# Six-layer macaron block on one core: GpSimd scales the normed rows behind the routed layers, kept rows go straight to their place, and the first combine loop is reordered

## The reference, cut to what matters

```
def _layernorm(x, axis=-1, eps=1e-05):
    m = jnp.mean(x, axis=axis, keepdims=True)
    v = jnp.var(x, axis=axis, keepdims=True)
    return (x - m) / jnp.sqrt(v + eps)
...
x = L0_attn_x
x = x + 0.5 * _L0_ffn_ref(_layernorm(x, axis=-1), ...)    # routed: 8 experts, top 2
x = x + _L0_attn_ref(_layernorm(x, axis=-1), ...)         # selective scan
x = x + 0.5 * _L0_ffn_ref(_layernorm(x, axis=-1), ...)    # routed again
x = x + 0.5 * _L1_ffn_ref(_layernorm(x, axis=-1), ...)    # soft: 64 experts, 32 slots each
x = x + _L1_attn_ref(_layernorm(x, axis=-1), ...)         # gated linear attention
x = x + 0.5 * _L1_ffn_ref(_layernorm(x, axis=-1), ...)    # soft again
```

## Time and profile before

| | before |
|---|---|
| median of 3 runs | 2232.11 us (2231.87 to 2232.35) |
| the profiled execution, own time | 2253.2 us |
| its span | 2251.4 us, 24417 instructions |
| mean granted TensorE clock | 0.954 of full speed |
| busy: TensorE, VectorE, ScalarE, GpSimd | 1869.9, 1666.6, 1184.8, 1230.3 us (83%, 74%, 53%, 55%) |
| chain that ended last, by engine | TensorE 35%, VectorE 32%, "issue" 15%, GpSimd 9%, ScalarE 4%, DMA 2% |
| of it, VectorE's scaling L1156 | 2% |

### The profile page before, as it was taken

One profiled execution on the slowest core, in us unless ns is written; L12 is line 12 of the kernel. 1 busy time (PEld: TensorE's weight loads), 2 busy tenths in 40 slices (PEclk: granted clock), 3 DMA queues, 4 the chain that ended last, 5 costly groups with the idle time before them and its releaser, 6 DMA issues.

```text
span 2251.4 us, 24417 instructions
## 1 busy us (share of the span) xinstructions
PE 1869.9 (83%) x6046; PEld 907.8 (40%) x6046; DVE 1666.6 (74%) x2166; ACT 1184.8 (53%) x2820; POOL 1230.3 (55%) x796
## 2 busy tenths in 40 slices
PE   4099686888888833986999999998987999999998
PEld 3067532333333521764333344443333433344443
DVE  5223488999999840327999967886687999958886
ACT  2322186555555332215999854332456999963332
POOL 3734307999999564552999800000785999900000
PEclk9999898999999956998999999999899999999999
DMA  7123293455455111325000000000650300000000
GB/s 261 50 84 103 94 154 113 169 178 176 169 176 176 64 60 51 107 71 169 1 0 0 1 1 1 0 0 0 186 141 19 94 0 0 0 1 5 9 9 14
DMA packets 102320, 163.63 MB, mean 73 GB/s; under 512 B 11008, under 2 KB 65843, under 8 KB 102113
## 3 DMA queue, kind: packets, MB, share of 16 engines
q1 hardware_dynamic: 94050, 146.41, 22.0%
q0 software_dynamic: 8192, 16.30, 2.0%
HBM read 125.09 MB, written 38.14 MB: 73 GB/s over the span
## 4 chain that ended last, share of the span: by engine, by line
PE 35%; DVE 32%; issue 15%; POOL 9%; ACT 4%; DMA 2%; another core or an unknown queue 1%; DVEq 1%; POOLq 0%; SPq 0%; ACTq 0%
PE ps L2005 10%; DVE arena L1461 5%; PE ps L1737 5%; PE ps L1750 5%; DVE arena L1523 5%; DVE arena L1467 5%; DVE arena L1459 4%; PE ps L1876 4%; PE ps L2033 3%; POOL arena L575 2%; POOL arena L638 2%; DVE arena L1529 2%; DVE arena L1406 2%; DVE stage L1156 2%; POOL arena L600 1%
## 5 line engine op out<-in xcount | busy, mean ns | idle before, releaser
L1951 PE MATMUL ps<-arena 128*128 128x512 f32 x512 | 250.6, 612 | 13.9 <-POOL arena L600 13.8
L608 POOL TENSOR_TENSOR arena<-arena 128x864 f32<-128x864 f32 x128 | 210.1, 1642 | 80.2 <-DVE arena L1459 77.4
L1942 PE MATMUL ps<-c_phiT,arena 128*128 128x512 f32 x512 | 244.1, 600 | 5.8 <-DVE arena L1461 3.8
L2005 PE MATMUL ps<-XT,c_phiT 128*128 (+1 forms) x512 | 243.4, 593 | 3.9 <-DVE arena L1499 3.9
L600 POOL TENSOR_TENSOR arena<-arena 128x1024 f32<-128x1024 f32 x128 | 246.6, 1928 | 0.0
L2033 PE MATMUL ps<-arena 128*128 128x512 f32 x512 | 227.7, 604 | 11.2 <-DVE arena L1529 11.2
L638 POOL TENSOR_TENSOR arena<-arena 128x1024 f32<-128x1024 f32 x32 | 63.6, 2000 | 299.2 <-DMA arena<-value_rows 299.2
L538 POOL DMA_INDIRECT token_outputs<-arena x128 | 124.3, 971 | 151.0 <-DVE arena L1298 112.0
L889 ACT ACTIVATE arena<-arena 128x32 f32<-128x32 f32 x640 | 195.7, 311 | 0.0
L1406 DVE TENSOR_TENSOR_SCAN arena<-ps,arena 128x1024 f32<-128x1024 f32 x84 | 187.9, 2274 | 6.4 <-POOL arena L570 6.2
L1876 PE MATMUL ps<-arena,c_ident 128*128 128x512 f32 x336 | 161.0, 601 | 28.3 <-POOL arena L575 28.3
(11 more groups left out here) (241 smaller groups left out, 3711.7 us busy)
## 6 DMA issues: line engine op xcount, KB each, us to landing
arena<-input_gates SPq DMA_DIRECT2D x128, 512.0 KB, 3.8
arena<-value_rows SPq DMA_DIRECT2D x32, 512.0 KB, 5.0
arena<-slot_inputs SPq DMA_DIRECT2D x32, 258.0 KB
arena<-in_L_ffn_w SPq DMA_DIRECT2D x32, 256.0 KB
arena<-token_outputs SPq DMA_DIRECT2D x16, 512.0 KB, 6.7
slot_inputs<-arena SPq DMA_DIRECT2D x1, 4128.0 KB, 13.4
slot_inputs<-zero SPq DMA_DIRECT2D x1, 4128.0 KB, 33.5
token_outputs<-arena SPq DMA_DIRECT2D x1, 4096.0 KB
```

Of the source, the lines that this page charges most:

```text
L608: pool.tensor_tensor(Ed[:, r, PSLOT * NA:].rearrange("p (n q) -> p n q", q=PSLOT), Lc[:, r, PSLOT * NA:].rearrange("p (n q) -> p n q", q=P ...
L1942: ins = pe.matmul(pbank(2 * h + c), xts[:, r // 2, :], phiT[:, at:at + CHUNK], start=True, stop=True)
L1951: ins = pe.matmul(pbank(4 + 2 * h + c), xns[:, r // 2, :], Dd[:, r, CHUNK * c:CHUNK * (c + 1)], start=start, stop=stop, skip_group_check=True)
L2005: ins = pe.matmul(pbank(t % 4), phiT[:, P * t:P * (t + 1)], xt(b, c), start=True, stop=without_m)
```

## The change

Three things are changed.

1. Kept rows (n = 0, 2, 3) are scaled straight into `XN[:, t, 0:D]`, TensorE turns them from there, and the 24 copies by ScalarE (L687) go, with the semaphore ln_keep; GpSimd's dispatch waits for ln_x instead.
2. Behind the routed layers (n = 1 and n = 3) the 32 scalings of each norm (8 chunks of 4 tiles) move from VectorE to GpSimd, behind its last scatter and, in layer 0, ahead of the clearing of `dts`.
3. In the combine loop of s = 0, VectorE's statistics use fixed slots and bn_aggr, `ln_apply` moves behind `weigh` and `tree`, TensorE's `ln_turn` behind `total` and `turn_y`, and ScalarE's `ln_copies` behind `finish`. In the loop of s = 1 `residual` moves behind `weigh` and `tree`.

```
@@ GpSimd, experts
-                    hold(pool, sem("ln_keep"), CHUNKS * m + c1)
+                    hold(pool, sem("ln_x"), 16 * m + c1)
...
                 store(E // 2 - 1, False, True)
 
+                n = 2 * m + 1
+                for c in range(CHUNKS):
+                    hold(pool, sem("ln_rstd"), 8 * n + c + 1)
+                    if m == 0 and c >= 2:
+                        pool.wait_ge(sem("ln_T"), 8 * n + c - 1)
+                    for j in range(PER_CHUNK):
+                        t = PER_CHUNK * c + j
+                        normed = XN[:, t, 0:D] if m else stage[:, c % 2, D * j:D * (j + 1)]
+                        ins = pool.tensor_scalar(normed, X[:, t, :], ln_s[:, 4, t:t + 1], ln_s[:, 7, t:t + 1], ALU.subtract, ALU.mult)
+                    ins.then_inc(sem("ln_x"), 1)
@@ ScalarE
-                if n in KEPT:
-                    hold(act, sem("ln_x"), 8 * n + c + 1)
-                    act.activation(XN[:, ds(4 * c, 4), 0:D], stage[:, h, :].rearrange("p (j d) -> p j d", d=D),
-                                   ACT.Copy).then_inc(sem("ln_keep"), 1)
...
                         copy_y(v - 1)
+                        finish(v)
                         if s == 0:
                             ln_copies(4, i - 1, c, 7)
-                        finish(v)
@@ VectorE, norms
-                if not (isinstance(v, int) and v < 2):
+                if n not in KEPT:
                     dve.wait_ge(sem("ln_T"), v - 1)
-                    if n in KEPT and not (isinstance(c, int) and c < 2):
-                        dve.wait_ge(sem("ln_keep"), 8 * KEPT.index(n) + c - 1)
...
+                    normed = XN[:, t, 0:D] if n in KEPT else stage[:, h, D * j:D * (j + 1)]
@@ VectorE, statistics (in a hardware loop seven operations before)
-                dve.tensor_tensor(two_mean, even(1), odd(1), ALU.add)
...
-                dve.tensor_tensor(var, var0, gap2, ALU.add).then_inc(sem("ln_var"), 1)
+                for t in range(at, at + PER_CHUNK):
+                    ins = dve.bn_aggr(ln_s[:, 4:6, t], stats[:, t, :])
+                ins.then_inc(sem("ln_var"), 1)
@@ VectorE, behind a routed layer
                     ln_statistics(2 * m + 1, grp)
-                    if grp:
-                        ln_apply(2 * m + 1, grp - 1, (grp - 1) % 2)
-                ln_apply(2 * m + 1, CHUNKS - 1, 1)
@@ VectorE, combine loop
                         less_m(v, c)
+                        weigh(v - 1, 1 - c, 1)
+                        tree(v, c)
                         if s == 0:
                             ln_apply(4, 2 * (i - 1) + c, c)
                         else:
                             residual(v - 2, i - 1, c)
-                        weigh(v - 1, 1 - c, 1)
-                        tree(v, c)
@@ TensorE, combine loop
                         combine(v - 1, 1 - c, False)
+                        total(v)
+                        turn_y(v - 1, False)
                         if s == 0:
                             ln_turn(4, 2 * (i - 1) + c, c, 7)
-                        total(v)
-                        turn_y(v - 1, False)
```

More of the change, by code:

```diff
@@ L672, in _, with ln_scale @@
             act.preload_act_table_set("natural_log_exp_and_others")
-            def ln_scale(n, c):
+            def ln_scale(n, c, ring=None):
+                at = 4 * (c if ring is None else ring)
                 hold(act, sem("ln_var"), 8 * n + c + 1)
-                act.activation(ln_s[:, 6, ds(4 * c, 4)], ln_s[:, 5, ds(4 * c, 4)], ACT.Ln, bias=eps[:, :]).then_inc(sem("ln_ln"), 1)
+                act.activation(ln_s[:, 6, at:at + 4], ln_s[:, 5, at:at + 4], ACT.Ln, bias=eps[:, :]).then_inc(sem("ln_ln"), 1)
                 hold(act, sem("ln_ln"), 8 * n + c + 1)
-                act.activation(ln_s[:, 7, ds(4 * c, 4)], ln_s[:, 6, ds(4 * c, 4)], ACT.Exp, scale=-0.5)\
+                act.activation(ln_s[:, 7, at:at + 4], ln_s[:, 6, at:at + 4], ACT.Exp, scale=-0.5)\
                     .then_inc(sem("ln_rstd"), 1)
@@ L933, in exp_T @@
                         if before and t == ST - 4:
-                            ln_scale(4, 2 * before[0] + before[1])
+                            ln_scale(4, 2 * before[0] + before[1], before[1])
                         hold(act, sem("LT"), ST * v + t + 1)
@@ L976, in soft @@
                     ln_copies(4, BATCH - 1, 0, 7)
-                    ln_scale(4, CHUNKS - 1)
+                    ln_scale(4, CHUNKS - 1, 1)
                     ln_copies(4, BATCH - 1, 1, 7)
@@ L1118, in _, with ln_statistics @@
             chain(dve.memset(XT[:, :, 0:CONV_PAD], 0.0))
-            def ln_statistics(n, c):
-                v = 8 * n + c
+            def ln_statistics(n, c, ring=None):
+                at = 4 * (c if ring is None else ring)
                 for j in range(PER_CHUNK):
-                    ins = dve.bn_stats(stats[:, ds(4 * c + j, 1), :].rearrange("p a b -> p (a b)"),
-                                       X[:, ds(4 * c + j, 1), :].rearrange("p a b -> p (a b)"))
-                if isinstance(v, int):
-                    ins.then_inc(sem("ln_step"), 3)
-                    dve.wait_ge(sem("ln_step"), 3 * v + 3)
-                    for t in range(4 * c, 4 * c + 4):
-                        ins = dve.bn_aggr(ln_s[:, 4:6, t], stats[:, t, :])
-                    ins.then_inc(sem("ln_var"), 1)
-                    return
-                ins.then_inc(sem("ln_step"), 1)
-                dve.wait_ge(sem("ln_step"), 3 * v + 1)
-                even, odd = (lambda j: stats[:, ds(4 * c, 4), j]), (lambda j: stats[:, ds(4 * c, 4), 3 + j])
-                two_mean, gap, m2, gap2, mean, var, _, _, var0 = (ln_s[:, j, ds(4 * c, 4)] for j in range(9))
-                dve.tensor_tensor(two_mean, even(1), odd(1), ALU.add)
-                dve.tensor_tensor(gap, even(1), odd(1), ALU.subtract)
-                dve.tensor_tensor(m2, even(2), odd(2), ALU.add).then_inc(sem("ln_step"), 1)
-                dve.wait_ge(sem("ln_step"), 3 * v + 2)
-                dve.scalar_tensor_tensor(gap2, gap, 0.25, gap, ALU.mult, ALU.mult)
-                dve.tensor_scalar(mean, two_mean, 0.5, None, ALU.mult)
-                dve.tensor_scalar(var0, m2, 1.0 / D, None, ALU.mult).then_inc(sem("ln_step"), 1)
-                dve.wait_ge(sem("ln_step"), 3 * v + 3)
-                dve.tensor_tensor(var, var0, gap2, ALU.add).then_inc(sem("ln_var"), 1)
+                    ins = dve.bn_stats(stats[:, at + j, :], X[:, ds(4 * c + j, 1), :].rearrange("p a b -> p (a b)"))
+                ins.then_inc(sem("ln_step"), 1)
+                hold(dve, sem("ln_step"), 8 * n + c + 1)
+                for t in range(at, at + PER_CHUNK):
+                    ins = dve.bn_aggr(ln_s[:, 4:6, t], stats[:, t, :])
+                ins.then_inc(sem("ln_var"), 1)
             def ln_apply(n, c, h):
@@ L1149, in ln_apply @@
                 dve.wait_ge(sem("ln_rstd"), v + 1)
-                if not (isinstance(v, int) and v < 2):
+                if n not in KEPT:
                     dve.wait_ge(sem("ln_T"), v - 1)
-                    if n in KEPT and not (isinstance(c, int) and c < 2):
-                        dve.wait_ge(sem("ln_keep"), 8 * KEPT.index(n) + c - 1)
+                at = 4 * (h if n == 4 else c)
                 for j in range(PER_CHUNK):
                     t = 4 * c + j
-                    ins = dve.tensor_scalar(stage[:, h, D * j:D * (j + 1)], X[:, ds(t, 1), :].rearrange("p a d -> p (a d)"),
-                                            ln_s[:, 4, ds(t, 1)], ln_s[:, 7, ds(t, 1)], ALU.subtract, ALU.mult)
+                    normed = XN[:, t, 0:D] if n in KEPT else stage[:, h, D * j:D * (j + 1)]
+                    ins = dve.tensor_scalar(normed, X[:, ds(t, 1), :].rearrange("p a d -> p (a d)"),
+                                            ln_s[:, 4, at + j:at + j + 1], ln_s[:, 7, at + j:at + j + 1], ALU.subtract, ALU.mult)
                 ins.then_inc(sem("ln_x"), 1)
@@ L1665, in ln_turn @@
                 for j in range(PER_CHUNK):
-                    ins = pe.transpose(pbank(bank)[:, P * j:P * (j + 1)], stage[:, h, P * j:P * (j + 1)], ident[:, :])
+                    normed = XN[:, 4 * c + j, 0:D] if n in KEPT else stage[:, h, P * j:P * (j + 1)]
+                    ins = pe.transpose(pbank(bank)[:, P * j:P * (j + 1)], normed, ident[:, :])
                 ins.then_inc(sem("ln_T"), 1)
```

4 lines of the change are left out of this document (2 added, 2 removed).

## The result

| | before | changed |
|---|---|---|
| median of 15 runs each | 2234.01 us (2230.89 to 2236.52) | 2236.85 us (2234.81 to 2238.53) |
| ratio to before, 95% interval | | 1.0015 (1.0009 to 1.0022) |
| the profiled execution, own time | 2253.2 us | 2236.5 us |
| its span | 2251.4 us | 2234.7 us |

The change makes the kernel 0.15% slower; 2209 was predicted, 1.0% faster. In a second comparison on another occasion the ratio was 1.0017 (1.0008 to 1.0026).

A forecast was written before the change was run, and what follows sets the result against it. TensorE and VectorE were taken to share the path, VectorE bounding the norm behind routed layer 0. Gains 9.8 + 5.4 + 4.0 + 3.6 = 22.8 us gave 2209.3 us; main-case range 2204 to 2216, wider range 2200 to 2225.

The forecast's parts named there:

- one input less makes the memset the nearer row, so I take 0.3: Norms behind routed layers: GpSimd's scaling of one 128-column tile estimated at 0.3 us, between 0.11 (memset) and 0.62 (additions).
- the formula for layer 1: Gain behind routed layer 1 if GpSimd sets the pace at s per scaling: 21.1 - 32s; layer 0's is 26.4 - 32s.
- Gain 9.8 behind layer 0: Norm behind routed layer 0: TensorE becomes the pace, first Silu at 280.75 against 290.5; 9.8 us, 3.3 from the memset stall.
- gain 5.4 behind layer 1: Norm behind routed layer 1: last turn and copy end at 1041.5 against 1046.97; 5.4 us (4.5 to 5.9).
- Loops, 4.0 and 3.6: Soft layers' combine loops: scaling (first) and residual (second) leave the path ahead of the tree; 4.0 and 3.6 us.
- The loops give nothing: Rival on the combine loops: TensorE refills the supposed path, so only 15.2 us remain, 2217; chance 0.04.
- Kept rows, nothing: Norms whose rows are kept: dropping 24 ScalarE copies of 0.63 us gains nothing, as ScalarE idles or copies beside TensorE's turn.
- the second rival: Slow GpSimd scaling in the norms behind routed layers: total gain 55.1 - 64s, 2258 at s = 1.27; chance 0.06.
- GpSimd is slow: Rival on the norms behind routed layers: scaling price s turns the gain to zero at 0.86, 2258 at 1.27; chance 0.06.
- GpSimd holds VectorE: Rival on the norms behind routed layers: each GpSimd scaling also stops VectorE; 8.1 us gained in all, 2224; chance 0.12.
- The stalls of the dispatch vanish: Rival on both routed layers' dispatch: the edit removes two waits of 7.26 us, 14.5 us more gained, 2195; chance 0.05.
- The memset beside the taps: Behind routed layer 0: memset now beside VectorE's convolution taps, counted as costing 0, with 2.4 us kept for the range.

The follow-up runs named there:

- residual_only: Kernel before, with only the residual moved behind the second product and the tree in the second soft layer's combine loop; 2226.12 us, ratio 0.9976.
- drain_ahead: Changed kernel, but GpSimd signals the end of routed layer 1 with its drain ahead of the 32 scalings; 2228.80 us against 2232.11, ratio 0.9986.
- wide_ahead: Changed kernel with two 128x512 tensor_tensor per chunk for GpSimd's scaling and its barrier drain ahead of the scalings; 2214.56 us against 2232.13, ratio 0.9924.
- wide: Changed kernel, but GpSimd scales a chunk by two tensor_tensor of 128x512 instead of four tensor_scalar of 128x128; 2241.74 us against 2257.45, ratio 0.9936.
- dve_both: Changed kernel with the scalings behind both routed layers on VectorE again; 2222.89 us, ratio 0.9960 to the kernel before.
- columns: Changed kernel, GpSimd scaling 64 columns per instruction behind layer 0 and 512 behind layer 1 (wrong scalars there), for the price alone; single run 2241.91 us.

## Why the prediction was wrong

- **The step that failed: "one input less makes the memset the nearer row, so I take 0.3".** Measured: 0.775 from one to the next. In the prediction's own sum this alone turns the 15.2 us of the two norms into a loss of 2.1. Of the 25.6 us between the forecast and the result that is 17.3; the drain (below) is 5.4 and the late projections about 2.5. The error lies in the choice of the near rows: a memset reads nothing, an addition has no scalars, and both bounds (0.11 and 0.62) were below the price. An instruction's form had a price that no row of before held, and the far bound of 1.27 was the only honest upper one. With 0.775 the formula for layer 1 is right: 21.1 - 32 x 0.775 is -3.7, and the scaling cost 3.6. The one for layer 0 gives 26.4 - 24.8 = 1.6 up to the first Silu. From the first addition to it the changed kernel took 31.5, against 32.5 in the profiled execution of before, but against 30.8 in residual_only, which has the code of before there. So the formula was 0.6 to 2.3 too favourable, since its rows came from an execution with a lower clock in that stretch. And 0.775 has a second cost that the formula leaves out, 2.4 to 2.8 us behind the first Silu (scan start minus first Silu: 81.9 against 79.1 to 79.5), where TensorE's projections start late and at the clock of 0.50; with wide scalings, at 1.00, this cost is gone (79.3).
- **The wait that was not seen: GpSimd's drain at the barrier.** The prediction let the soft layer start 2.2 us after the last scaling. To ask what is queued behind the scalings on GpSimd would have found it: `stage_end` stood there, and in the trace of before GpSimd's drain was done 27 us ahead of ScalarE's last copy (1019.79 and 1046.97), so it cost nothing. 5.4 us, shown by drain_ahead.
- **Gain 9.8 behind layer 0** came out as a loss of 3.4 to 3.8, **gain 5.4 behind layer 1** as a loss of 9.0. With both causes mended (wide_ahead) the same two stages gain 6.1 and 2.3 against residual_only, which has the old code there: the mechanism (VectorE relieved, TensorE nearly the pace) was right, and the size was too large by 3.7 and 3.1. Of the 3.7, 1.7 is the low clock in the execution that the forecast started from. In both stages the turns come 2.4 apart and not 2.2, with waits for GpSimd between them, which makes about 1 us of each, and the first turn, which was to follow the sums at once, waits 1.1 (wide) and 0.8 (wide_ahead) for GpSimd. What remains behind layer 1, over 1 us, isn't taken apart.
- **Loops, 4.0 and 3.6:** right, and for the reason given. From chunk to chunk the first loop gives 0.6 to 0.7 five times and 1.03 at the last, 4.1 in all; the second 0.6 six times, 3.5. The stages (3.6 to 4.6, and 3.5 to 5.2) and the runs (5.4) hold the clock of the last chunk besides. So the rival "The loops give nothing" fell.
- **Kept rows, nothing:** no experiment isolates them. dve_both and residual_only, of one occasion, differ by them and by the first loop; they are 3.2 us apart, of which the loop's stage makes 3.7. So the kept rows gave nothing beyond the 2 us or so to which such a difference is known. The lengths of the dispatch are the same within 0.4 us in residual_only, which has the copies, and in the changed kernel, which hasn't (86.2 and 86.2 us from the first to the last dispatch of layer 1).
- **Slips in the sums,** which change nothing: 273.3 + 1.92 is 275.2 and not 275.4, and the second rival has 15.0 for the two gains, which are 15.2.
- **Rivals.** "GpSimd is slow" was the right one, with 0.06. In the prediction's sum the change turns slower from s = 0.86, so the measured 0.775 alone would have left a gain of 5.5. With the drain (5.4) and the late projections (2.5) the sum turns at 0.74, and 0.775 gives 2.4 slower: this rival needed the other two costs to come true. "GpSimd holds VectorE" didn't happen: VectorE's additions beside the scalings took 0.69. "The stalls of the dispatch vanish" took them for the kernel's. They are absent from the changed kernel's trace, but from residual_only's as well, and on that occasion the kernel before took the 2232 that the forecast started from; so there was nothing to gain. The memset beside the taps was rightly counted at nothing (4.12 and 4.07 for six). The Trainium skill, "SBUF — State Buffer", section "Who interferes with whom", had both: no hold of taps by a memset that only writes, but contention of two-input VectorE instructions with a GpSimd instruction that reads. The trace agrees there too: GpSimd's last scaling, at 276.00 beside the first taps (275.68), took 1.61 instead of 0.79, and three of 64 columns beside taps in the run columns took 1.35 to 1.48 instead of 0.57.
- **The warning of a page was taken too lightly.** The Trainium skill, "GPSIMD Engine Reference", section "Engine selection", calls one-input elementwise work near line rate. Measured, the 128-column scaling takes three times VectorE's step of 0.25. Its advice, to leave such work on VectorE, was right here for four tensor_scalar a chunk; with two wide instructions a chunk the move paid, 6.1 and 2.3 us in the two stages.

Put together from the stages, against residual_only's code: + 3.5 + 8.7 - 4.3 and, for the second loop, - 3.5 to - 5.4, is + 2.5 to + 4.4; measured + 2.8 and + 4.3.

## What to carry to other kernels

An instruction that the trace doesn't show in its very form (engine, operation, where the scalars come from, width) has no near bound from its neighbours; time it alone before you move work by it. When work moves to an engine that was done early, its barrier signal moves too: look at what that engine still has to do after its last instruction, and signal ahead of the work where other semaphores already guard it. Two wide instructions in place of four narrow ones, and the signal ahead of them, made the whole change worth 17 us instead of a loss of 4; against the kernel that has all but this move (dve_both) the move went from a loss of 13 to a gain of 8.

## What was unexpected of the hardware

- GpSimd's drain behind routed layer 1 ends 7.3 us after its last instruction, whether that was a tensor_scalar (1030.13 to 1037.42) or a scatter (in wide_ahead 984.08 to 991.33), where ScalarE's ends about when its copy does (0.63 from issue to end). But not each drain of GpSimd costs this. At the end of the selective scan it is 7.3 as well (750.51 to 757.79, behind an addition); at the end of its work in each soft layer it is 0.08 (1279.58 to 1279.66, behind an addition too), and so in all traces. What the slow ones have in common is that GpSimd has issued indirect DMAs since its drain before, and ahead of the fast ones it hasn't. No run tests that this is the cause.
- GpSimd's tensor_scalar with two operations and scalars in memory: 0.57, 0.78 and 2.07 us for 64, 128 and 512 columns; a two-input instruction of 512 columns with a broadcast input 1.04.
- The dispatch of both routed layers had waits of 6.3 to 7.4 us each in all kernels of one occasion, and in the profiled execution of before, and in no trace of two other occasions; what makes them stays open.
